# Reading the coming layer's code inside the running operation of a data-dependent layer loop

## The reference

```
x = x + conv_block_0(ln(x))          # shift conv, adder conv, twice
t = to_tokens(x)                     # 4 x 784 tokens of 32 channels
t = t + layers(ln(t))                # 33 layers, see below
x = from_tokens(t)
x = x + quantised_conv_block(ln(x))
x = x + spectral_mixer(ln(tokens(x)))

def step(h, p):                      # one of the 33 layers
    op = argmax(h[0, 0, :19])        # first token decides
    y = softmax(q k^T / sqrt(32)) v wo      # weights p[...][op]
    h = where(attn_mask[layer, op], y, h)
    z = relu(h w1 + b1) w2 + b2             # 32 -> 128 -> 32
    h = where(ffn_mask[layer, op], z, h)
```

## Time and profile before

| | us |
|---|---|
| median of 3 runs | 344.49 (344.34, 344.49, 348.11) |
| profiled execution, device time | 343.95 |
| its span, first to last instruction | 342.2 |
| start of the first FFN's token column on PE | 150.97 |
| start of the attention's projections | 162.40 |
| start of the second FFN's token column | 218.77 |
| first square of the layer norm behind the layers (ACT) | 226.67 |

### The profile page before, as it was taken

The page is one execution under the profiler, slowest core; times in us unless marked ns, Lnnn a source line. Parts: engine busy times, 40 slices in busy tenths (PEclk is TensorE's granted clock), DMA queues, the critical chain, the costliest instruction groups (busy, mean ns, idle before and its releaser), DMA issues.

```text
span 342.2 us, 11955 instructions
## 1 busy us (share of the span) xinstructions
PE 322.1 (94%) x5173; PEld 202.4 (59%) x5173; DVE 249.4 (73%) x510; ACT 188.6 (55%) x214; POOL 21.5 (6%) x48
## 2 busy tenths in 40 slices
PE   8899799999999999958999999989899999999995
PEld 7436437763333333434465334446589999999984
DVE  2797999999999999544694877647657675564444
ACT  3871898887889894324584867641333323223221
POOL 4573000000000000300000000000000000000000
PEclk9999999999999999999999999999999999999999
DMA  5701820000000003700000000000023000000001
GB/s 181 234 17 20 310 99 2 2 1 2 2 2 2 2 2 111 268 14 19 3 0 2 3 1 2 2 5 1 2 61 87 7 4 4 4 5 4 6 4 50
DMA packets 12243, 13.20 MB, mean 39 GB/s; under 512 B 6026, under 2 KB 10908, under 8 KB 12184
## 3 DMA queue, kind: packets, MB, share of 16 engines
q1 hardware_dynamic: 11208, 9.17, 9.0%
q0 software_dynamic: 832, 3.00, 2.6%
q10 hardware_dynamic: 144, 0.20, 0.2%
HBM read 10.73 MB, written 0.40 MB: 33 GB/s over the span
## 4 chain that ended last, share of the span: by engine, by line
PE 54%; DVE 31%; SPq 7%; issue 4%; ACT 2%; DVEq 1%; DMA 1%; ACTq 0%
PE PS L1088 54%; DVE pool_ L877 18%; SPq L274 3%; DVE pool_ L965 1%; DVE TMP L841 1%; DVE TMP L973 1%; SPq L268 1%; DMA WA2R<-in_wa2r 1%; SPq L277 1%; SPq L279 1%; DVE RSC L648 1%; DVE pool_ L874 1%; SPq L281 1%; DVE MSC L790 1%; ACT pool_ L544 0%
## 5 line engine op out<-in xcount | busy, mean ns | idle before, releaser
L1088 PE MATMUL PS<-pool_,CON 128*32 128x392 f32 (+2 forms) x1320 | 111.4, 493 | 0.6 <-ACT pool_ L544 0.2
L1088 PEld LDWEIGHTS PS<-pool_,CON 128*32 128x32 f32 (+1 forms) x1320 | 49.0, 110 | 60.8 <-issue 43.7
L495 ACT ACTIVATE pool_<-TMP,WA 128x3136 f32<-128x3136 f32 x26 | 75.3, 2924 | 11.0 <-PE PS L1088 10.8
L877 DVE TENSOR_SCALAR pool_<-TMP,WA 128x3136 f32<-128x3136 f32 x44 | 79.4, 1845 | 0.1
L594 ACT ACTIVATE pool_<-PS 128x272 f32<-128x272 f32 x64 | 25.4, 398 | 56.7 <-PE PS L1088 56.6
L1061 DVE TENSOR_TENSOR pool_<-PS,pool_ 128x128 f32<-128x128 f32 x64 | 18.6, 290 | 35.4 <-PE PS L1088 32.7
L1088 PE MATMUL PS<-HE,WS 128*32 128x136 f32 (+1 forms) x768 | 36.7, 317 | 0.2 <-ACT WS L586 0.2
L1088 PE MATMUL PS<-pool_,WS 128*32 128x136 f32 (+1 forms) x768 | 36.7, 316 | 0.0
L1088 PEld LDWEIGHTS PS<-pool_,WS 128*32 128x32 f32 x768 | 28.7, 109 | 3.0
L1088 PEld LDWEIGHTS PS<-HE,WS 128*32 128x32 f32 x768 | 28.3, 110 | 3.6 <-issue 0.6
L1088 PE MATMUL PS<-pool_,TMP 128*32 128x128 f32 x512 | 29.0, 272 | 0.0
(11 more groups left out here) (261 smaller groups left out, 372.3 us busy)
## 6 DMA issues: line engine op xcount, KB each, us to landing
pool_<-in_pho SPq DMA_DIRECT2D x1, 3144.0 KB, 10.7
HE<-in_phe SPq DMA_DIRECT2D x1, 3136.0 KB, 12.5
QZ<-CW SPq DMA_DIRECT2D x12, 98.0 KB, 2.4
CW<-in_cw POOLq DMA_DIRECT2D x2, 576.0 KB, 4.8
CON<-in_con POOLq DMA_DIRECT2D x1, 732.5 KB, 5.4
out_y<-Y SPq DMA_DIRECT2D x1, 392.0 KB, 2.4
CQ<-in_ws SPq DMA_DIRECT2D x16, 9.0 KB
MPP<-in_mpp POOLq DMA_DIRECT2D x1, 256.0 KB, 2.9
```

Of the source, the lines that this page charges most:

```text
L495: a.activation(unit, window(n // CQ), ACT.Abs, bias=WA2[:, n:n + 1], scale=-1.0).then_inc(s["act_unit"], 1)
L877: v.tensor_scalar(unit, window(n // CQ), WA2[:, n:n + 1], None, ALU.max).then_inc(s["dve_unit"], 1)
L1088: return t.matmul(out_, lhsT, rhs, start=start, stop=stop, skip_group_check=True)
```

## The change

- **Coming code.** PE and ACT get a register `coming` and a function `next_code`. In a step with an FFN they wait for `decided`, signal `read_on` and load KINT ahead of the second group (h = 1); `step` ends with register operations alone. A step with attention only reads behind it, as before. PE's `wait ffn_h` moves from the step's end to where H is next read (the projections, the token column, the tail).
- **First code.** PE reads it inside `norm(1)`, between the variance products and `rest(1)`; DVE reads it there behind the reciprocal.
[...]
- **Token row.** It stands behind products u = 0, 1 instead of 0 to 3.
- **Evictions.** ACT evicts u = 0, 1, 2, 3, 4, 6; DVE evicts 5 and 7 and runs `decide` first. The group h = 0 now waits for ACT's fourth eviction.
- **CEN products.** In an FFN they stand between the groups h = 0 and h = 1, behind the evictions of banks 4 and 5.
- **Dummy products.** 3 instead of 8 ahead of the projections, both in bank 7, and the wait for `ln_out` stands behind them; the 8 of `further` are gone (they are in the third copy of the step, which does not run here).

```diff
-WARM = dict(inputs=6, means=4, squares=2, deviations=3, scaled=4, sums=2, copies=9, evictions=3, shifts=1, relus=3, further=8, rises=2, weights=4, projections=8)
+WARM = dict(inputs=6, means=4, squares=2, deviations=3, scaled=4, sums=2, copies=9, evictions=3, shifts=1, relus=3, further=8, rises=2, weights=4, projections=3)
 OPW = 1024
...
             a.reg_mov(na, 0); a.reg_mov(nf, 0)
-            ops = a.alloc_register("a_ops")
-            a.reg_mov(ops, 0)
+            ops = a.alloc_register("a_ops"); coming = a.alloc_register("a_coming")
+            a.reg_mov(ops, 0); a.reg_mov(coming, 0)
+            def next_code(more):
+                a.wait_ge(s["decided"], a.snap(ops, min_val=0, max_val=2 * NB) + more)
+                a.sem_inc(s["read_on"], 1)
+                a.load(coming, KINT[0:1, 0:1], bass_reorder=False)
             def step(c):
...
                     a.activation(TOK[:, :], PS[:, 7, 0:1], ACT.Relu, bias=B1S).then_inc(s["tok_hid"], 1)
-                    for u in (0, 2, 3, 4, 6):
+                    for u in (0, 1, 2, 3, 4, 6):
                         a.wait_ge(s["ffn_h1"], k * 8 + (u + 1))
...
                     for h in range(2):
+                        if h:
+                            next_code(2)
                         a.wait_ge(s["ffn_out"], k * 2 + (h + 1))
...
                     a.reg_add(nf, nf, 1); a.reg_add(ops, ops, 1)
-                a.wait_ge(s["decided"], a.snap(ops, min_val=1, max_val=2 * NB) + 1)
-                a.sem_inc(s["read_on"], 1)
-                a.load(code, KINT[0:1, 0:1], bass_reorder=False)
-                a.reg_mov(code, a.snap(code) & (OPW - 1))
+                with a.If((c & 2) < 1):
+                    next_code(1)
+                a.reg_mov(code, a.snap(coming) & (OPW - 1))
...
             decide(1, 6)
-            norm(1, X1, lambda h: half(H, h))
+            code = v.alloc_register("v_code"); na = v.alloc_register("v_na"); nf = v.alloc_register("v_nf")
+            def first_code():
+                v.wait_ge(s["decided"], 1)
+                v.load(code, KINT[0:1, 0:1], bass_reorder=False)
+                v.reg_mov(code, v.snap(code) & (OPW - 1))
+            norm(1, X1, lambda h: half(H, h), after=first_code)
...
-            code = v.alloc_register("v_code"); na = v.alloc_register("v_na"); nf = v.alloc_register("v_nf")
-            v.wait_ge(s["decided"], 1)
-            v.load(code, KINT[0:1, 0:1], bass_reorder=False)
-            v.reg_mov(code, v.snap(code) & (OPW - 1))
             ops = v.alloc_register("v_ops")
...
                     v.tensor_copy(B2C[:, :], B2S).then_inc(s["bias_kept"], 1)
-                    for u in (1, 5, 7):
+                    decide(v.snap(ops, min_val=0, max_val=2 * NB) + 2, 7)
+                    for u in (5, 7):
                         v.wait_ge(s["ffn_h1"], k * 8 + (u + 1))
                         v.tensor_scalar(HIDT[:, u, :], bank(u % 7), B1S, 0.0, ALU.add, ALU.max).then_inc(s["hid_dve"], 1)
-                        if u == 1:
-                            decide(v.snap(ops, min_val=0, max_val=2 * NB) + 2, 7)
                     v.reg_add(nf, nf, 1); v.reg_add(ops, ops, 1)
...
-            def norm(k, src, ready=None, summed=None):
+            def norm(k, src, ready=None, summed=None, between=None):
                 if k == 1:
...
                 last.then_inc(s["ln_var"], 1)
+                if between:
+                    between()
                 rest(k)
...
             ffn_mark = t.mark_branch_hint_location()
-            norm(1, X1, "x1_ready")
-            t.wait_ge(s["ln_out"], 4)
-            t.wait_ge(s["decided"], 1)
             code = t.alloc_register("t_code"); na = t.alloc_register("t_na"); nf = t.alloc_register("t_nf")
-            t.load(code, KINT[0:1, 0:1], bass_reorder=False)
-            t.reg_mov(code, t.snap(code) & (OPW - 1))
-            t.reg_mov(na, 0); t.reg_mov(nf, 0)
-            ops = t.alloc_register("t_ops")
+            ops = t.alloc_register("t_ops"); coming = t.alloc_register("t_coming")
             built = []
-            t.reg_mov(ops, 0)
+            def first_code():
+                t.wait_ge(s["decided"], 1)
+                t.load(code, KINT[0:1, 0:1], bass_reorder=False)
+                t.reg_mov(code, t.snap(code) & (OPW - 1))
+                t.reg_mov(na, 0); t.reg_mov(nf, 0); t.reg_mov(ops, 0); t.reg_mov(coming, 0)
+            norm(1, X1, "x1_ready", between=first_code)
+            def next_code(more):
+                t.wait_ge(s["decided"], t.snap(ops, min_val=0, max_val=2 * NB) + more)
+                t.sem_inc(s["read_on"], 1)
+                t.load(coming, KINT[0:1, 0:1], bass_reorder=False)
             exit_marks = []
...
-                with (t.If((c & 1) > 0) if built else far_unless(t, c & 1, ffn_mark)):
+                with (t.If((c & 1) > 0) if built else far_unless(t, c & 1, ffn_mark, True)):
                     k = t.snap(na, min_val=0, max_val=NB)
                     t.wait_ge(s["zeroed"], 4)
-                    keep_warm(WARM["projections"])
+                    keep_warm(WARM["projections"], b=7)
                     t.wait_ge(s["att_w"], k * 16 + 16)
+                    t.wait_ge(s["ffn_h"], t.snap(nf, min_val=0, max_val=NB) * 2 + 1)
+                    if not built:
+                        t.wait_ge(s["ln_out"], 4)
                     bridge()
...
                     if not built:
-                        keep_warm(WARM["weights"])
+                        keep_warm(WARM["weights"], b=7)
                     t.wait_ge(s["ffn_wa"], k * 16 + 16)
+                    t.wait_ge(s["ffn_h"], k * 2 + 1)
+                    if not built:
+                        t.wait_ge(s["ln_out"], 4)
                     mm(PS[:, 7, 0:1], W1R[0:C, 0:HID], H[0:C, 0:1]).then_inc(s["tok_mm"], 1)
-                    for h in range(2):
-                        for b in range(NIMG):
-                            u, q = 4 * h + b, slice(32 * b, 32 * b + 32)
-                            if u == 6:
-                                t.wait_ge(s["decided"], t.snap(ops, min_val=0, max_val=2 * NB) + 1)
-                            if u == 7:
-                                t.wait_ge(s["hid_act"], k * 5 + 1)
-                            mm(bank(u % 7), W1R[q, 0:HID], half(H, h)[q]).then_inc(s["ffn_h1"], 1)
-                        if h == 0:
+                    for u in range(8):
+                        h, b = divmod(u, 4)
+                        q = slice(32 * b, 32 * b + 32)
+                        if u == 6:
+                            t.wait_ge(s["decided"], t.snap(ops, min_val=0, max_val=2 * NB) + 1)
+                        if u == 7:
+                            t.wait_ge(s["hid_act"], k * 6 + 1)
+                        mm(bank(u % 7), W1R[q, 0:HID], half(H, h)[q]).then_inc(s["ffn_h1"], 1)
+                        if u == 1:
                             t.wait_ge(s["ffn_wb"], k * 16 + 16)
...
                     for h in range(2):
-                        t.wait_ge(s["hid_act"], k * 5 + 2 * h + 3)
-                        t.wait_ge(s["hid_dve"], k * 3 + 2 * h + 1)
+                        if h:
+                            t.wait_ge(s["hid_act"], k * 6 + 5)
+                            mm(bank(4), CEN[:, :], half(X1, 0), True, False)
+                            t.wait_ge(s["hid_dve"], k * 2 + 1)
+                            mm(bank(5), CEN[:, :], half(X1, 1), True, False)
+                            next_code(2)
+                        t.wait_ge(s["hid_act"], k * 6 + 2 * h + 4)
+                        if h:
+                            t.wait_ge(s["hid_dve"], k * 2 + 2)
                         for b in range(NIMG):
...
                     t.reg_add(nf, nf, 1); t.reg_add(ops, ops, 1)
-                f, o = t.snap(nf, min_val=0, max_val=NB), t.snap(ops, min_val=1, max_val=2 * NB)
-                built.append(o)
-                if len(built) == 3:
-                    keep_warm(WARM["further"])
-                for h in range(2):
-                    mm(bank(4 + h), CEN[:, :], half(X1, h), True, False)
-                t.wait_ge(s["ffn_h"], f * 2 + 1)
-                t.wait_ge(s["decided"], o + 1)
-                t.sem_inc(s["read_on"], 1)
-                t.load(code, KINT[0:1, 0:1], bass_reorder=False)
-                t.reg_mov(code, t.snap(code) & (OPW - 1))
+                with t.If((c & 2) < 1):
+                    for h in range(2):
+                        mm(bank(4 + h), CEN[:, :], half(X1, h), True, False)
+                    next_code(1)
+                built.append(c)
+                t.reg_mov(code, t.snap(coming) & (OPW - 1))
...
+            t.wait_ge(s["ffn_h"], t.snap(nf, min_val=0, max_val=NB) * 2 + 1)
             for h in range(2):
...
```

## The result

By the ratio of the times after to those before the change made the kernel faster by 0.7%, inside the 2% that the prediction took as no clear change: the ratio is 0.9927, 95% interval 0.9904 to 0.9949, or 2.5 us (1.8 to 3.3). The ratio leaves out nine of the 20 executions after as slow ones (346.7 to 349.5 us, mean clock 0.972 to 0.985), and over all 20 the means are 345.2 us after and 345.3 before. The medians of 20 executions each are 343.89 us after and 345.08 before. The profiled execution took 342.91 us with a span of 341.1, against 343.95 and 342.2. Forecast were 340.3 and a range of 338.2 to 342.5: the sign was right, but the median lies 1.4 us above the range.

What follows compares the result with a forecast made beforehand. PE and DVE were taken to fill 85% of the chain that bounds the kernel, "issue" 11%. Projections -5.4 and hand-over +1.3 give -4.1 us on 343.95: 339.85, so a predicted median of 340.3, range 338.2 to 342.5.

Steps and rivals of the forecast that it cites:

- the first decision: First FFN: DVE, not PE, sets when the code is written, at 152.23 instead of 154.98, 2.75 us earlier.
- the projections: Behind the first FFN: they start at 156.9 to 157.0 instead of 162.40, 5.4 us earlier.
- W4R last: Ahead of the projections: W4R lands at 156.45 and ends last, 0.35 us behind PE's dummy products.
- the 0.2 taken for it: Layer norm ahead of the first FFN: PE's moved read makes H 0.2 us later, 0.4 at most.
- the jump waits for its code: Rival, PE's jump ahead of the first FFN: it comes before its target; projections slip 0.7 to 2 us; chance 0.17.
- 1.7 us that I gave PE in hand: First FFN: PE's token row would be ready by 149.6, leaving PE 1.7 us of slack.
- 1.8 us later: Second FFN: h = 1 starts at 224.62 instead of 222.82, with the CEN products now ahead of it.
- The later h = 0: Second FFN: h = 0 waits for ACT's fourth eviction and starts at about 222.39, 0.8 us later.
- 1.3 us lost: Hand-over from the second FFN to the layer norm: ACT's squares come later, 1.3 us lost (0.1 to 1.6).
- a new stall for code on DVE or ACT: Closing sign: if the profile after shows such a stall, the number falls; no size or chance given.
- the clock: Rival: the clock falls at the first FFN's waits, slowing attention; 8 us at the lower level give 348; chance 0.05.
- the forecast's -4.1: Whole kernel: -5.4 us for the projections and +1.3 for the hand-over, on the profiled execution's 343.95.

Runs made afterwards that it cites:

- e10: Kernel after the change with PE's first read of the code behind the layer norm again; ratio 1.0028 to the kernel before.
- e9: Kernel after the change with DVE's first read of the code behind H again; ratio 0.9959 to the kernel before.
- e2: Kernel after the change with the FFN's two CEN products moved back behind h = 1; ratio 0.9919 to the kernel before.
- e6: Kernel after the change with 27 instructions fewer in the never-run third copy of ACT's step; median 340.07 us, ratio 0.9900 to the kernel before.
- e1: Kernel after the change with ACT announcing its exit from the steps ahead of time; median 339.99 us, ratio 0.9861 to the kernel before.
- e5: Kernel before the change with 59 small ACT operations more in the never-run third copy of ACT's step; ratio 1.0075 to the kernel before.
- e4: Kernel before the change with three dummy products ahead of the projections instead of eight; ratio 0.9945 to the kernel before.
- e7: Kernel after the change with eight dummy products on PE in its wait for ACT's squares; ratio 0.9964 to the kernel before.
- e8: Kernel after the change without the alignment of the FFN's code on PE; ratio 0.9968 to the kernel before.

## Why the prediction was wrong

**Right: the first decision and the projections.** Code 3.0 us earlier (forecast 2.75), projections 5.25 earlier (forecast 5.4), W4R last by little (e10's wait ends at 156.74; forecast 156.45), DVE and not PE as the bound (e9). H was not late at all; the 0.2 taken for it is most of what 2.75 lacks.

**Right only by its cover: PE's jump.** The rival "the jump waits for its code" came true as a mechanism (2.39 us instead of 0.38, with the block landing inside it) and not as a loss. Of the 1.7 us that I gave PE in hand it used all but 0.4: the row was done at about 150.68, DVE wanted it at 151.05.

**Right: CEN.** "1.8 us later" for h = 1 against the old kernel was 1.7 (5.75 less 4.05), and e2 has 1.28 for the products alone. The later h = 0, forecast at 0.8, is 0.58 (3.44 behind the token column instead of 2.86); no run takes it apart.

**Wrong: the hand-over's "1.3 us lost".** It failed in its ACT part, "without the load of 0.28 and its wait, but with a branch over the block for attention-only steps (0.24), 1.03". That sum took for granted that the code behind ACT's exit is loaded, because it was before. The last sentence of the prediction named the hole ("a new stall for code on DVE or ACT"), but no rival and no price stood for it. The stretch forecast at 1.03 measured 3.10 us. Where the code is there, the same stretch is 0.87 (e6) or 1.08 (e1): the term was sound, its condition was not. By my count of ACT's program (no profile shows it), from the exit branch to the table load it is some 180 instructions in the kernel before, 189 in the one after, 162 in e6 and some 240 in e5; the code is late at 189 and 240, in time at 162 and 180. Whether the distance decides or where the target lies within a block of code, these runs don't tell. The new instructions of `next_code` and the sixth eviction stand in the third copy too, which never runs, and push the target away. The diff showed them; I costed only those that run.

**Wrong: the clock.** The rival put a fall at the first FFN, and its chance of 0.05 rested on one row, the hole of 3.05 us that cost nothing. That row was the exception: behind the same hole the clock is at 0.50 in e4 and e5. The change took that hole down to 1.32 us (0.58 to 1.69 in its edits), and in all ten profiles with the change the clock is 1.00 there; how much of the measured gain is this, no run shows. The fall came at the tail, behind a wait that the first error made, and cost 1.3. At the tail it fell behind all five waits of 3.03 to 3.20 us, and behind the old hole in two profiles of three; the third shows that a hole of this length (3.05 us) need not bring the fall.

The sum as measured: -5.25 for the projections, +3.20 for the first square, -0.29 because from the first square to the last output it takes 4.84 (e7, clock up) instead of 5.13 (226.67 to 231.80), as the second square now follows the first by 0.37 instead of 0.66, +1.29 for the clock: -1.05. With ACT's code in time (e6) the span is 338.1, 4.1 us below the profiled execution before: the forecast's -4.1. That its median of 340.07 meets the forecast 340.3 is in part luck: it is of four executions, and its ratio of 0.9900 is 3.5 us. The forecast's median also counted from an execution of before at a clock of 1.000, which is rare.

## What to carry to other kernels

Where a program branches, code that never runs can have a price (1.99 us in e5): count what an edit adds between a jump and its target on every engine, and read each such jump's length in the profile before calling it fixed. A jump moved earlier can arrive ahead of its own code, as PE's did here (2.39 us at 145.0, 0.47 at 146.2 in e10): read its length before counting the gain (whether an earlier announcement would have helped, no run tried). Do not judge a risk by one profiled execution: the row that spoke against the clock's fall was the exception. And price a stall on a side engine twice: once for what waits, and once for what the wait does to TensorE's clock (here 3.20 us and 1.3).

## What was not expected of the hardware

- A late jump costs about 2 us over a loaded one on both engines: ACT 1.99 (e5 against before), PE 1.89 to 2.76 against 0.38 to 0.47. An announced one can still be late (PE at 144.7 to 145.1, in nine profiles; in the kernel after its announcement runs at 137.0). Why the announced code was late there stays open: only the jump's time was varied, not the announcement's.
- The granted clock also falls to the lower level inside attention, in five of the 13 profiles (e1, e4, e8 to e10), where PE's rows show it busy 95 to 100% of the time: in e1's profile its mean from 170 to 190 us is 0.74, and the span is 3.6 to 4.5 us above those of its executions at 1.00. No run here shows why.
